# Fewer semaphore waits on TensorE's queue in the last stage of a two-layer network kernel

## The reference

```python
x = x + r * wkv @ Wo
yn = _ln(x, ln2_g, ln2_b)
yp = _shift(yn)
kk = jnp.square(jax.nn.relu((0.5 * yn + 0.5 * yp) @ Wfk))   # Wfk: 1024 x 4096
rr = jax.nn.sigmoid(yn @ Wfr)                               # Wfr: 1024 x 1024
return x + rr * (kk @ Wfv)                                  # Wfv: 4096 x 1024
```

## Time and profile before

| | |
|---|---|
| median of 3 runs (lowest, highest) | 11947.3 us (11945.35, 11951.69) |
| the profiled execution, its own time | 11953.15 us |
| span of the slowest core in it (all cores) | 11951.6 us (11929.0 to 11951.6) |
| TensorE matmuls busy | 7424.2 us, 62% |
| VectorE, ScalarE busy | 3706.7 us, 31%; 2449.8 us, 20% |
| mean granted clock of TensorE, cores 0 to 7 | 0.706 to 0.758 of full speed |

### The profile page before, as it was taken

How to read it: one execution, slowest core, us unless ns; L and a number is a source line. 1 busy time by engine, 2 the same in 40 slices (tenths; PEclk the granted TensorE clock), 3 DMA queues, 4 the chain that set the end, 5 groups by cost and what they waited for, 6 DMA issues and landing times. The chain is left out here.

```text
span 11951.6 us, 118359 instructions; the slowest of 8 cores (11929.0 to 11951.6 us)
## 1 busy us (share of the span) xinstructions
PE 7424.2 (62%) x24170; PEld 2509.6 (21%) x24170; DVE 3706.7 (31%) x5460; ACT 2449.8 (20%) x4533; POOL 501.6 (4%) x835
## 2 busy tenths in 40 slices
PE   1100485867758677586867755758484848484848
PEld 1000121212212222121212211313131313131313
DVE  2641214142240422314132153242414141415141
ACT  0110241422314133141422311011111010101110
POOL 3543000000000000000000000000000000000000
PEclk9999757576675857657576677878796979696979
DMA  5427301011110201101011112313131414141414
GB/s 89 142 102 103 44 17 54 1 41 30 34 37 2 64 6 39 32 15 57 1 41 30 34 39 61 102 55 108 50 114 44 118 40 120 38 120 39 122 46 121
DMA packets 552961, 702.58 MB, mean 59 GB/s; under 512 B 219578, under 2 KB 281730, under 8 KB 552066
## 3 DMA queue, kind: packets, MB, share of 16 engines
q1 hardware_dynamic: 457090, 636.23, 18.4%
q0 software_dynamic: 95232, 58.77, 3.6%
HBM read 687.94 MB, written 67.11 MB: 63 GB/s over the span
## 5 line engine op out<-in xcount | busy, mean ns | idle before, releaser
L1299 ACT ACTIVATE l_e<-l_psA,l_mcols 128x1024 bf16<-128x1024 f32 x1024 | 1140.8, 1114 | 1378.6 <-PE l_psA L1289 1272.2
L2166 PE MATMUL l_pb<-l_A,l_wts 128*128 128x256 bf16 x4096 | 1000.8, 274 | 111.4 <-DMA l_wts<-wfk_c 59.9
L1289 PE MATMUL l_psA<-l_qpk 64*128 64x512 bf16 x2048 | 966.6, 623 | 38.5 <-DVEq L764 19.8
L2200 PE MATMUL l_pso<-l_rs 128*128 128x256 bf16 x4096 | 981.7, 271 | 11.9 <-DMA l_rs<-wfv_c 1.2
L1315 PE MATMUL l_psB<-l_e,l_vt 128*64 128x512 bf16 x2048 | 977.5, 633 | 4.0 <-ACTq L764 4.0
L1601 PE MATMUL l_psA<-l_h,l_w2s 128*128 128x512 bf16 x2048 | 562.3, 412 | 443.9 <-DVEq L764 389.1
L2175 DVE TENSOR_SCALAR l_ev<-l_pb 128x256 f32<-128x256 f32 x512 | 217.5, 425 | 1977.6 <-PE l_pb L2166 1943.0
L1928 PE MATMUL l_pb<-l_mixb,l_wts 128*128 128x512 bf16 x1536 | 464.4, 436 | 502.7 <-DVEq L764 385.3
L1198 PE MATMUL l_psA<-l_xnq,l_w1s 128*128 128x512 bf16 x2048 | 510.6, 399 | 243.8 <-DMA l_w1s<-w1T_c 201.8
L2180 ACT ACTIVATE l_rs<-l_ev 128x256 bf16<-128x256 f32 x512 | 213.1, 416 | 1971.5 <-PE l_pso L2200 1685.3
L1345 DVE TENSOR_TENSOR l_z<-l_zc 128x16 f32<-128x16 f32 x32 | 5.6, 175 | 1880.6 <-ACTq L764 1876.4
(11 more groups left out here) (340 smaller groups left out, 7465.0 us busy)
## 6 DMA issues: line engine op xcount, KB each, us to landing
l_wts<-wfk_c SPq DMA_DIRECT2D x2048, 64.0 KB, 1.9
l_rs<-wfv_c SPq DMA_DIRECT2D x512, 256.0 KB, 2.6
l_w1s<-w1T_c SPq DMA_DIRECT2D x1024, 64.0 KB, 1.9
l_w2s<-w2T_c SPq DMA_DIRECT2D x512, 128.0 KB, 2.7
wst<-L_ffn_w SPq DMA_DIRECT2D x64, 512.0 KB
wst<-L_ffn_w SPq DMA_DIRECT2D x128, 128.0 KB
wstS<-L_ffn_w SPq DMA_DIRECT2D x128, 128.0 KB, 2.9
l_wqs<-wqT_c SPq DMA_DIRECT2D x256, 64.0 KB, 1.9
```

The lines of the kernel that those rows point to most:

```text
L1289: lambda t, pp=pp, a=a, Rb=Rb, kc=kc, sh=sh: t.matmul(sh[:, (kc % 2) * CH:(kc % 2) * CH + CH], qpk[pp][a * 64:a * 64 + 64, 128 * Rb:128 * ...
L1299: lambda s, a=a, Rb=Rb, rnd=rnd, pp=pp, sh=sh: s.activation(out=e_sb[a][:, rnd * 1024:(rnd + 1) * 1024], in_=sh, func=AF.Exp, scale=1.0 / ...
L2166: lambda t, mb=mb, buf=buf, dc=dc, toff=toff: t.matmul(pb[mb][:, 0:256], wfks[buf][:, dc * 128:(dc + 1) * 128], ymt[:, dc * CH + toff:dc * ...
L2200: lambda t, f2=f2, buf=buf, oc=oc: t.matmul(pso[:, oc * 256:(oc + 1) * 256], wfvs[buf][:, oc * 128:(oc + 1) * 128], kks[buf], start=(f2 == ...
```

## The change

Three lists of waits change, all on TensorE. Before, every one of the eight matmuls of a group in the gate and in the K part of the loop waited for the weight load and for the activations (`ynt` or `ymt`), and every one of the eight in the V part for the square and for the load of Wfv; the bank's wait stood at the first one only. Now the first matmul of each group carries all of them and the other seven none. The groups are the same, so are matmuls, transfers, buffers and increments. In each chunk this is 8 groups of the gate, 2 x 32 of K and 2 x 32 of V.

```diff
@@ the gate, Wfr
             for dc in range(DC):
-                wl = [(sWS[buf], ws_t), (sDV, yn_done)] + (bw(mb) if dc == 0 else [])
+                wl = ([(sWS[buf], ws_t), (sDV, yn_done)] + bw(mb)) if dc == 0 else []
@@ K, Wfk
                     for dc in range(DC):
-                        wl = [(sWS[buf], ws_t), (sDV, ym_done)] + (bw(mb) if dc == 0 else [])
+                        wl = ([(sWS[buf], ws_t), (sDV, ym_done)] + bw(mb)) if dc == 0 else []
@@ V, Wfv
                     for oc in range(DC):
-                        wl = [(sAC, kk_ready[f2]), (sWV[buf], od_t)]
+                        wl = [(sAC, kk_ready[f2]), (sWV[buf], od_t)] if oc == 0 else []
                         if f2 == 0 and oc == 0:
                             wl += fw("outst")
```

## The result

The changed kernel takes 11348.7 us (median of 8 runs, 11339.5 to 11379.9) against 11958.2 for the kernel before beside it (8 runs): ratio 0.9497, interval 0.9485 to 0.9508, so 609.5 us less. Forecast were 657 less and 11290; 11348.7 is inside the range of 11160 to 11420. The profiled execution has a span of 11346.2 us on its slowest core, core 7.

A forecast was written before the change was run, and what follows sets the result against it. Waits on TensorE's queue bound the loop, SyncE's issuing next at 2.68 us a step. The profiled 11953.2 less 653 (loop) and 4 (gate) gives 11296, less 5.9 to the runs' median: 11290 us, range 11160 to 11420.

The forecast's parts named there:

- The pace (a): K and V groups of the loop: 0.108 us per unwaited matmul, a group in 1.03 us instead of 1.9.
- The bound before: K and V loop before the change: two waits per matmul pace TensorE, each further wait costing 0.10 us, hiding 256 columns.
- SyncE (b): Loop after the change: SyncE's issuing of loads sets the step, taken as 2.68 us, lower end 2.38.
- The way round (c): Wfk loads through two buffers: 3.67 us from K's end to K(fs+2), so a step of at least 2.35 us, covered.
- Traffic (d): Loads in the loop: rate rises from 131 to 194 GB/s, which is to be had since the trace shows 225.
- The half chunk (e): Loop per half chunk: 8.2 + 29 x 2.68 = 85.9 us instead of 126.7, saving 653 us over 16.
- The gate (f): Receptance groups of line 2134: shorter groups save 4 us over the 8 chunks, bounds 0 and 8.
- the loads slow down: Rival: loop loads slow under their own traffic, steps of 2.85 to 3.3 us, 11370 to 11600 us; chance 0.14.
- Clock at 1.2 GHz in the loop: Rival: TensorE pauses for loads and its clock drops, step 3.64 us, time 11770 us; chance 0.03.
- the slower case: Rival: load slowing carried on until the step passes today's 3.96 us, for example 4.10 and 12010 us; chance 0.02.
- The clock of 0.81: Loop on TensorE: denser columns could bring core 3's granted clock to every core, TensorE's own step 2.52 us, under 2.68.
- SyncE's waits in the loop near zero: Sign expected in the changed profile: SyncE hardly waits in the loop, where it waited 41.1 us of a half chunk.

## Why the prediction was right, and where it was not

- The pace (a): right. 0.108 forecast, groups of 1.03 us forecast and measured; and the wait's 0.10 holds in the run with one wait (0.130 against the 0.134 of line 1261).
- The bound before: right, and shown from the other side by the kernel with its waits kept, 1.0005.
- SyncE (b): a clean step of 2.38 forecast, 2.40 in the timeline. Its own mean was taken as 2.68 and is (1430.1 - 141.0)/512 = 2.52 in the changed kernel, 2.58 with the third Wfk buffer. Too high by 0.1 to 0.16, and so it was in the kernel before: from one step's first slab to the next, waits taken off, its trace has 2.53 in the mean. The 127 us that 2.68 came from hold 5.3 us after SyncE's last load of the half chunk (issued by 9974.67), which are not its work.
- The way round (c): this is the step that failed. "3.67 in all. Two steps are that plus K's 1.03, so a step is at least (3.67 + 1.03)/2 = 2.35. Near SyncE's bound, and below it." Over the 480 steps it takes 4.45 us in the mean: 0.30 from K's end to the first slab (0.13 in the median), 1.36 to the last slab and 2.79 from there to the matmul, where the forecast's 3.67 is 0.13, 1.27 and 2.27. (4.45 + 1.08)/2 = 2.77 is the measured 2.76 by definition, whatever binds: K's length and the time to the next K but one make two steps. That the way round does bind is read from its ends. In 62% of the 480 steps the first slab goes out within 0.2 us of K's end, and in 78% K starts 0.35 us behind its last slab's landing, against under 1% in the kernel before. And the 4.45 gave the steps of two other kernels, with V's waits alone removed and with one wait back, within 0.05. The largest piece, 0.52, is nearly all landing: all slabs have landed 2.40 us behind the last one's issue, 1.92 in the load that the forecast took (issued 9850.95, landed 9852.87). The loop's own traffic I had put into a rival and priced at no more than SyncE's bound. So the bound I named was not the one that sets the end, and the number came out near by luck: one bound was taken too high and the other too low. With 2.52 in place of 2.68 the same sum gives 11217, 132 us under the measured time.
- Traffic (d): right, 186 GB/s where 194 were forecast, and 222 is to be had.
- The half chunk (e): 8.2 + 29 x 2.68 = 85.9 forecast, 89.4 measured. From K(2) to K(31) the step is 2.75, 29 x 0.07 = 2.0 us more. From K(0) to K(2) it is 5.87 us instead of 4.70, 1.2 more: the second K waits for its load, and in the second half chunk of every chunk, behind a pause of 21 us, the first groups run at 1.2 GHz. The end, from K(31) on, is 3.81 instead of 3.51. Saved 600 instead of 653.
- The gate (f): 4 forecast, bounds 0 to 8; 5.8 on the cores of the two profiles, 7.8 in the mean over six.
- The range: by the prediction's own sum a step of 2.38 gives 11151 and one of 2.93 gives 11407, where it wrote 11160 and 11420. The slips of 9 and 13 us change nothing.
- The rivals: "the loads slow down" is what happened, at a step of 2.76 and not the 2.85 to 3.3 of its case. Clock at 1.2 GHz in the loop: in 39 of 1024 groups. Nothing of the slower case. The clock of 0.81 came in 6 of 128 half chunks, by pairs of cores and neither on a whole die nor steadily, so the 2.52 that the prediction kept ready for all of the loop was hardly used.
- Of the signs, "SyncE's waits in the loop near zero" was wrong: 0.28 us a step. The rate of 186 GB/s is just under its 190 to 215, and 6 of the 16 half chunks are over 90 us.

## What to carry to other kernels

When the columns of a matmul are fewer than the queue's work for its waits, semaphore waits already satisfied set the pace: put all of a group's waits on its first matmul, and look for equal paces at unequal column counts to find such a place. What a cover that goes away hid must then be priced at the new rate: landing times of the slow kernel are too short for the fast one. Where two bounds lie within a few per cent, removing one shows little: two transfers fewer gave 0.3%, more buffers 0.4%, both 2.0%.

## What the runs showed of the hardware that was not expected

- A wait on TensorE's queue runs beside the matmul's columns: 256 columns cost 0.108 us with no wait, 0.130 with one, 0.233 with two.
- Moving half of the traffic to a second issuing queue, and with it to an earlier moment, made it worse: from the last slab to its matmul 3.23 us instead of 2.64, time up by 135 us, at an unchanged number of bytes.
- Landing grows with the rate and with what is in flight: 64 KB in 2.0 us at 131 GB/s and 2.4 at 186; 128 KB in 2.9, and 4.0 in the kernel with 222 GB/s and three buffers, where the step is still the shortest of all, 2.29.
- The granted clock of 0.81 to 0.82 comes and goes in loops of this density, by pairs of cores and for whole half chunks: in 72, 14 and 6 of 128 half chunks in three kernels, the densest of which had the 14.
